# One pool of seven PSUM banks for scores, maxima and all other matmuls, in place of separate sets of two, two and three

## The chip, the cores and the metric

The kernel runs on one core of one Trainium2 chip. The metric is the device time of one execution in microseconds (us); lower is better. A core has a matrix engine (PE, whose weight loads are shown as PEld), a vector engine (DVE), a scalar engine (ACT), a general engine (POOL), DMA queues fed by SP, and an accumulation memory (PSUM) of eight banks, 512 fp32 values by 128 partitions each, that PE writes and DVE and ACT read.

## The reference, cut to what matters

Four blocks one after another work on `x` (4 batches, 256 rows, 160 columns) with a context of 512 rows of 96. Seven attentions are computed in all:

```python
x = L0(x, ctx)   # cross attention, 20 heads of 8, 512 keys
x = L1(x, ctx)   # LN, self attention (20 heads, 256 keys); LN, cross attention (512 keys); LN, gated feed forward 160 -> 2*640 -> 160
x = L2(x, ctx)   # 8 heads of 20: attention to 508 context rows, plus a small attention of 96 rows to x, fed to another with 4 keys
x = L3(x, ctx)   # as L1

# each attention
sim = einsum('bhid,bhjd->bhij', q, k) * scale
out = einsum('bhij,bhjd->bhid', softmax(sim), v)
```

## The kernel before, in words

**Staging.** The attentions make six phases (`PHASES`), each over four batches `b`. Within a phase and batch the heads are worked in groups of four, a *quad* (`quads`, 116 in all). For a quad with 512 keys the steps are:

- `max`, eight per quad: PE computes scores with queries as rows (one matmul of 512 columns, or two of 256 in self attention) into a bank `mx_ps` (line 911), and DVE reduces them to row maxima (line 1337). 720 in all.
- `negm`, then `mtr`: DVE negates the maxima (lines 1351 and 1352), PE transposes them (line 925), and DVE adds them to the queries as extra rows (line 1361), so that the next scores come out with the maximum subtracted.
- `st`, a *slot*, eight per quad: PE computes scores of two heads with keys as rows (two matmuls of 256 columns, line 889) into a bank `st_ps`, and ACT takes the exponential into one of eight `probs` buffers (line 1177). 736 in all.
- `pv`, four per quad: PE multiplies two slots' probabilities with the values into the bank `pv_ps` (eight matmuls of nine weight columns, line 949); `oev`: ACT copies the sum out (line 1186).

`max` and `st` use 64 of PE's 128 rows each: heads of one half of a quad lie on rows 0 to 63 and the others on rows 64 to 127, and two such matmuls of different halves run at the same time. `pv` splits the columns of PE into four. All other steps use the whole array: projections, transposes of keys and queries (`k_tr`, line 994; `q_tr`, line 1053), the way out of an attention (`o_nat`, `o_tr`, `o_proj`) and the feed forward (`ff_g`, `ff_a`, `ff_o`). There are 640 of these with a bank, the 116 `mtr` among them, and they take a bank in turn from three, `sp_ps`; ACT or DVE empties it.

**Banks.** `st_ps` has two banks (`N_ST`), `mx_ps` two (`N_MX`), `sp_ps` three (`N_SP`), each set used in strict rotation, and `pv_ps` one.

**What sets the order.** Nothing is ordered at run time: a planner (`simulate`) runs when the kernel is built and writes down one order of all 2,995 steps, which every engine then follows through its own queue, with semaphores between them. The planner keeps a clock per engine. At each point it takes, of the first steps of several streams (slots; maxima; `mtr`; `pv`; background work), the one that PE could start first, and between equal times the one with the earlier due time. It reckons 95 ns (`MODE`) for a change between the three shapes of PE (rows, columns, full), 210 ns (`HANDOFF`) from engine to engine, 60 + 1.05 ns a column for DVE and 60 + 0.834 ns a column for ACT. A step that needs a bank can't start before the planned end of the reader of the step before it in that bank. Maxima run some 8 to 16 slots ahead of the slots of their quad (`M_LEAD` is 8), and a slot also needs that the `pv` of eight slots before is done.

Of the kernel before, what the change touches and what calls it, by code (L numbers as in the profile page):

```python
# [62 lines left out]
N_ST = 2  # L63
N_SP = 3
N_MX = 2
# [132 lines left out]
def plan():  # L198
# [61 lines left out]
    order = simulate(quads, slots, due, stages)  # L260
    return order, quads, slots
# [103 lines left out]
def simulate(quads, slots, due, stages):  # L365
# [38 lines left out]
    def data_needs(step):  # L404
# [81 lines left out]
    done, order, uses, maxes = {}, [], [], []  # L486
# [3 lines left out]
    while any(heads) or any(stages) or any(map(any, active)) or any(active_low):  # L490
        for p in range(3):
            if not any(active[p]) and stages[p] and (stages[p][0][0] is None or stages[p][0][0] in done):
                active[p] = [list(x) for x in stages[p].pop(0)[1]]
        best = None
        for li in heads + active[0] + active[1] + active[2] + active_low:
            if not li:
                continue
            step = li[0]
            need = needs(step)
            if any(x not in done for x in need):  # L500
                continue
            lock = takes_buffer(step)
            if lock and held.get(lock[0]) not in (None, lock[1]):
                continue
            start = max([done[x] for x in need], default=0)
            if step[0] in SPARE and len(uses) >= N_SP:
                if uses[-N_SP] not in done:
                    continue
                start = max(start, done[uses[-N_SP]])
            if step[0] == "max" and len(maxes) >= N_MX:  # L510
                start = max(start, done[maxes[-N_MX]])
            key = (max(start, pe_free(step)), due.get(step)) if cost(step, quads)[0] else (max(start, clock["pe"]), (-10**6, 0, 0))
            if best is None or key < best[0]:
                best = (key, start, li, step)
        key, start, li, step = best
        li.pop(0)
        order.append(step)
        lock = takes_buffer(step)
        if lock:
            held[lock[0]] = None if lock[2] else lock[1]  # L520
        pe, after = cost(step, quads)
        t = start
        if pe:
            begin = max(start, pe_free(step))
            mode, t = shape(step), begin + pe
            if mode == "rows":
                lanes[lane(step)], clock["pe"] = t, begin + (pe / 2 if step[0] == "st" else 0)
            else:
                lanes, clock["pe"] = [t, t], t
        for eng, ns in after:  # L530
            t = clock[eng] = max(t + HANDOFF, clock[eng]) + ns
        done[step] = t + (DMA_LATENCY if step[0] == "kdma" else HANDOFF)
        if step[0] in LOW:

            uses.append(("low", step))
            active_low.append([("low", step)])
        elif step[0] in SPARE:
            uses.append(step)
        if step[0] == "max":
            maxes.append(step)  # L540
    return order
# [6 lines left out]

LOW = {"kv_proj", "qkv_proj", "q_proj", "ca_q"}
# [3 lines left out]
    "scores_full": {"st"}, "probs_ready": {"st"}, "max_full": {"max"}, "max_taken": {"max"}, "negm_ready": {"negm"},  # L553
# [19 lines left out]
def build(nc, io):  # L573
    order, quads, slots = plan()

    value, seen, turn, uses = {}, {}, {}, 0
    for step in order:
# [7 lines left out]
        if step[0] in SPARE:  # L585
            turn[step] = (uses % N_SP, uses // N_SP)
            uses += 1

    def slot_value(name, s):
        return value[name, ("st", s)]  # L590

    with ExitStack() as ctx:
# [6 lines left out]

        st_ps = [ctx.enter_context(nc.psum_tensor(f"st_ps{i}", [P, 512], F32)) for i in range(N_ST)]  # L600
        mx_ps = [ctx.enter_context(nc.psum_tensor(f"mx_ps{i}", [P, 512], F32)) for i in range(N_MX)]
        pv_ps = ctx.enter_context(nc.psum_tensor("pv_ps", [P, 512], F32))
        sp_ps = [ctx.enter_context(nc.psum_tensor(f"sp_ps{i}", [P, 512], F32)) for i in range(N_SP)]
# [69 lines left out]
        spare_full = [sem(f"spare_full{i}") for i in range(N_SP)]  # L673
        spare_taken = [sem(f"spare_taken{i}") for i in range(N_SP)]
# [65 lines left out]
        def taken(eng, step):  # L740

            b, k = turn[step]
            eng.wait_ge(spare_taken[b], k + 1)
# [19 lines left out]
        with nc.Block() as block:  # L763
# [31 lines left out]
            def _(pe):  # L795

                pe.wait_ge(s_warm, 1)
                for _ in range(WARM_UP):
                    pe.matmul(st_ps[0][:, :], probs[:, 0, 0:P], probs[:, 0, :], start=True, stop=True)
# [10 lines left out]
        with nc.Block() as block:  # L810
            @block.sync
            def _(sp):
# [14 lines left out]
                for step in order:  # L827
                    if step[0] == "kdma":
# [6 lines left out]
                        if before is not None:  # L835

                            sp.wait_ge(S["scores_full"], quads[before]["slots"][-1] + 1)
# [23 lines left out]
            def _(pe):  # L861
                def take(step):

                    b, k = turn[step]
                    if k:
                        pe.wait_ge(spare_taken[b], k)
                    return sp_ps[b], spare_full[b]
# [6 lines left out]
                for step in order:  # L874
                    kind = step[0]
                    if kind == "st":
# [7 lines left out]
                        if s >= N_ST:  # L884

                            pe.wait_ge(S["probs_ready"], slot_value("probs_ready", s - N_ST))
                        kr = chunk_rows(a["nk"], c)
                        for i, h in enumerate(sl["heads"]):
                            mm = pe.matmul(st_ps[s % N_ST][0:kr, i * a["nq"]:(i + 1) * a["nq"]],  # L889
                                           key_op(n, h)[:, c * P:c * P + kr], query_rows(u, b, h),  # L890
                                           start=True, stop=True)
                        mm.then_inc(S["scores_full"], 1)
                    elif kind == "max":
# [12 lines left out]
                        o = value["max_full", step] - 1  # L906
                        if o >= N_MX:
                            pe.wait_ge(S["max_taken"], o - N_MX + 1)
                        tt = 0 if t == TQ else t
                        for j, h in enumerate(heads):  # L910
                            mm = pe.matmul(mx_ps[o % N_MX][0:rows, j * a["nk"]:(j + 1) * a["nk"]],  # L911
                                           query_rows(u, b, h)[:, tt * P:tt * P + rows], key_op(n, h)[:, 0:a["nk"]],
                                           start=True, stop=True)
                        mm.then_inc(S["max_full"], 1)
# [13 lines left out]
                    elif kind == "pv":  # L928
# [8 lines left out]
                        pe.wait_ge(S["probs_ready"], slot_value("probs_ready", mine[-1]))  # L937
# [208 lines left out]
            def filled(eng, step):  # L1146

                b, k = turn[step]
                eng.wait_ge(spare_full[b], k + 1)
                return sp_ps[b], spare_taken[b]  # L1150
# [8 lines left out]
            def _(act):  # L1159
# [6 lines left out]
                for step in order:  # L1166
                    kind = step[0]
                    if kind == "st":
                        s = step[1]
                        a = ATT[slots[s]["u"]]  # L1170
                        act.wait_ge(S["scores_full"], s + 1)
                        if s >= N_P:
# [4 lines left out]
                        nc.scalar.activation(probs[0:kr, s % N_P, 0:w], st_ps[s % N_ST][0:kr, 0:w], ACT.Exp,  # L1177
                                             scale=float(a["dh"]) ** -0.5).then_inc(S["probs_ready"], 1)
# [30 lines left out]
                    elif kind == "x_keys":  # L1209
# [4 lines left out]
                        act.wait_ge(spare_full[turn[prev][0]], turn[prev][1] + 1)  # L1214
# [74 lines left out]
            def _(dve):  # L1289
# [38 lines left out]
                for step in order:  # L1328
                    kind = step[0]
                    if kind == "max":  # L1330
# [4 lines left out]
                        o = value["max_full", step]  # L1335
                        dve.wait_ge(S["max_full"], o)
                        nc.vector.tensor_reduce(mx[b][0:rows, t, heads[0]:heads[-1] + 1:heads[-1] - heads[0] or 1],  # L1337
                                                mx_ps[(o - 1) % N_MX][0:rows, 0:a["hpm"] * a["nk"]].rearrange("p (h k) -> p h k", k=a["nk"]),
                                                AX.X, ALU.max).then_inc(S["max_taken"], 1)
                    elif kind == "negm":  # L1340
# [6 lines left out]
                        dve.wait_ge(S["max_taken"], value["max_taken", ("max", n, len(quads[n]["items"]) - 1)])  # L1347
# [185 lines left out]
```

## Time and profile before

| | us |
|---|---|
| median of 3 runs (1029.38 to 1034.0) | 1033.69 |
| the profiled execution | 1032.42 |
| its span, first to last instruction | 1030.3 |
| PE busy | 975.2 |
| DVE busy | 680.7 |
| ACT busy | 672.4 |
| POOL busy | 55.1 |

Busy is the time in which an engine had at least one instruction under way. Matmuls are pipelined, and the end of each is modelled, so that short stops of PE lie inside its busy time; the start times of its instructions and the idle time of PEld tell more.

### The profile page before, as it was taken

What the parts mean: (1) busy time and instruction counts of PE and PEld (TensorE: products, weight loads), DVE (VectorE), ACT (ScalarE), POOL (GpSimd) and SP (SyncE); (2) the same over time, 40 slices, a digit from 0 to 9 for tenths busy, and PEclk for the clock granted to TensorE, in tenths of its full rate; (3) what the DMA queues carried; (4) which work ended last, traced back from release to release, by engine and by line L of the source; (5) the groups of instructions that cost most, each with busy time, mean ns of one, the idle gap of its engine ahead of it and who ended that gap; (6) DMA issues with size and microseconds to landing.
All of it is one profiled execution on the core that took longest, in us unless ns stands there. A gap on an engine that the chain in (4) does not pass through costs nothing.

```text
span 1030.3 us, 21206 instructions
## 1 busy us (share of the span) xinstructions
PE 975.2 (95%) x7808; PEld 642.1 (62%) x7808; DVE 680.7 (66%) x1607; ACT 672.4 (65%) x1416; POOL 55.1 (5%) x92
## 2 busy tenths in 40 slices
PE   4999999999999999999999999999999999989878
PEld 2865565566666657676667766665666666665636
DVE  2168878787776875757675677577587875848531
ACT  1567777676777677767776577576577775756541
POOL 2000000000000001000000000000000000000000
PEclk7589999999999999999999999799699998998975
DMA  7111111101112001011000300001011101011000
GB/s 182 45 24 42 24 30 42 25 23 24 27 26 48 22 22 32 22 32 32 12 2 2 78 1 1 22 17 26 18 26 42 35 19 38 22 33 26 18 1 6
DMA packets 25324, 30.04 MB, mean 29 GB/s; under 512 B 9204, under 2 KB 16824, under 8 KB 25064
## 3 DMA queue, kind: packets, MB, share of 16 engines
q1 hardware_dynamic: 25224, 28.69, 12.0%
q8 instruction: 64, 1.05, 0.4%
q14 instruction: 36, 0.29, 0.1%
HBM read 7.04 MB, written 0.66 MB: 7 GB/s over the span
## 4 chain that ended last, share of the span: by engine, by line
PE 87%; DVE 5%; issue 3%; ACT 2%; DMA 1%; SPq 0%; POOL 0%; ACTq 0%; DVEq 0%; POOLq 0%
PE pv_ps L949 18%; PE mx_ps L911 16%; PE st_ps L889 13%; PE sp_ps L871 8%; PE sp_ps L872 7%; PE sp_ps L994 6%; PE sp_ps L976 4%; PE sp_ps L925 4%; PE sp_ps L1053 3%; DVE mx L1337 3%; PE sp_ps L1065 3%; PE sp_ps L1104 2%; ACT probs L1177 1%; DMA ctx_n<-in_ctx 1%; PE sp_ps L1011 1%
## 5 line engine op out<-in xcount | busy, mean ns | idle before, releaser
L1337 DVE TENSOR_REDUCE mx<-mx_ps 128x1 f32<-128x512 f32 (+3 forms) x720 | 465.9, 684 | 151.2 <-PE mx_ps L911 148.5
L1177 ACT ACTIVATE probs<-st_ps 128x512 f32<-128x512 f32 x736 | 395.3, 587 | 149.1 <-PE st_ps L889 142.6
L911 PE MATMUL mx_ps<-ring,qT 64*128 64x512 f32 (+1 forms) x800 | 221.0, 435 | 11.9 <-issue 6.6
L949 PE MATMUL pv_ps<-probs,v 128*9 128x256 f32 (+2 forms) x2944 | 225.4, 391 | 1.1 <-ACT oT L1186 0.7
L889 PE MATMUL st_ps<-qT,ring 64*128 64x256 f32 x1280 | 208.9, 309 | 6.2 <-ACT probs L1177 2.9
L889 PEld LDWEIGHTS st_ps<-qT,ring 64*128 64x128 f32 x1280 | 152.8, 191 | 48.9 <-ACT probs L1177 30.7
L911 PEld LDWEIGHTS mx_ps<-ring,qT 64*128 64x128 f32 x800 | 103.3, 193 | 108.5 <-DVE mx L1337 52.0
L949 PEld LDWEIGHTS pv_ps<-probs,v 128*9 128x9 f32 (+2 forms) x2944 | 50.5, 91 | 62.2 <-issue 17.7
L1228 ACT ACTIVATE kdense<-sp_ps 128x512 fp32r<-128x512 f32 (+2 forms) x116 | 59.2, 542 | 24.1 <-PE sp_ps L994 23.3
L994 PE MATMUL sp_ps<-identr,ks 128*128 128x128 f32 (+1 forms) x416 | 68.3, 299 | 0.1
L994 PEld LDWEIGHTS sp_ps<-identr,ks 128*128 128x128 f32 (+1 forms) x416 | 58.1, 207 | 12.0 <-issue 8.9
L1186 ACT ACTIVATE oT<-pv_ps 128x256 f32<-128x256 f32 x108 | 41.6, 385 | 30.5 <-PE pv_ps L949 30.3
L1361 DVE TENSOR_TENSOR qT<-sp_ps,qT 128x256 fp32r<-128x256 f32 (+1 forms) x108 | 47.0, 435 | 20.1 <-PE sp_ps L925 20.0
L1164 ACT ACTIVATE ks<-sp_ps 128x320 fp32r<-128x320 f32 x80 | 35.5, 443 | 35.4 <-PE sp_ps L872 17.7
L1303 DVE TENSOR_TENSOR ks<-sp_ps,ks 128x160 fp32r<-128x160 f32 x80 | 24.1, 316 | 50.0 <-ACT v L1200 39.6
L925 PEld LDWEIGHTS sp_ps<-identr,mn 128*128 128x128 f32 (+1 forms) x248 | 38.7, 199 | 28.0 <-issue 23.5
L925 PE MATMUL sp_ps<-identr,mn 128*128 128x128 f32 (+1 forms) x248 | 53.9, 306 | 1.1 <-DVE mn L1352 1.0
L871 PE MATMUL sp_ps<-hT_out,wb 80*128 80x256 f32 x160 | 53.7, 420 | 1.2 <-ACT hT_out L1238 1.2
L872 PE MATMUL sp_ps<-hT_out,wb 80*128 80x256 f32 x160 | 52.2, 411 | 0.0
L1469 POOL TENSOR_SCALAR rstd<-mv 128x2 f32<-128x2 f32 x24 | 5.2, 217 | 802.9 <-DVE mv L1375 802.9
L1411 DVE TENSOR_TENSOR x<-sp_ps,xb 128x320 f32<-128x320 f32 x32 | 15.7, 491 | 43.3 <-PE sp_ps L872 22.5
L1053 PE MATMUL sp_ps<-identr,qs 128*128 128x128 f32 (+1 forms) x248 | 42.0, 304 | 0.0
(151 smaller groups left out, 1094.4 us busy)
## 6 DMA issues: line engine op xcount, KB each, us to landing
ring<-kdense SPq DMA_DIRECT2D x240, 64.0 KB, 2.0
ring<-kdense SPq DMA_DIRECT2D x160, 32.0 KB, 1.8
wb<-in_w_blk SPq DMA_DIRECT2D x2, 1400.0 KB, 9.1
wd<-in_w_down SPq DMA_DIRECT2D x2, 400.0 KB, 9.6
ctx_n<-in_ctx SPq DMA_DIRECT2D x4, 192.0 KB, 2.6
x<-in_x SPq DMA_DIRECT2D x4, 160.0 KB, 2.9
bias<-in_bias SPq DMA_DIRECT2D x1, 640.0 KB
out_rows<-x SPq DMA_DIRECT2D x4, 160.0 KB, 1.9
```

Source lines behind the costliest of these rows:

```text
L871: pe.matmul(out, lhs[:, 0, :], rhs[:, 0, :], start=True, stop=False)
L872: return pe.matmul(out, lhs[:, 1, :], rhs[:, 1, :], start=False, stop=True)
L889: mm = pe.matmul(st_ps[s % N_ST][0:kr, i * a["nq"]:(i + 1) * a["nq"]], key_op(n, h)[:, c * P:c * P + kr], query_rows(u, b, h), start=True, ...
L911: mm = pe.matmul(mx_ps[o % N_MX][0:rows, j * a["nk"]:(j + 1) * a["nk"]], query_rows(u, b, h)[:, tt * P:tt * P + rows], key_op(n, h)[:, 0:a ...
L925: mm = pe.matmul(bank[:, k * a["nq"] + i * P:k * a["nq"] + i * P + rows], m, identr[0:rows, 0:rows], start=True, stop=True)
L949: mm = pe.matmul(pv_ps[32 * j:32 * j + a["dh"] + 1, 0:a["nq"]], v, probs[0:kr, s % N_P, i * a["nq"]:(i + 1) * a["nq"]], start=(c == 0), st ...
L994: mm = pe.matmul(bank[:, k * SQ + t * P:k * SQ + t * P + kr], ks[0:kr, t, g * of(u):(g + 1) * of(u), :].rearrange("p h s -> p (h s)"), ide ...
L1053: mm = pe.matmul(bank[:, k * nq + i * P:k * nq + i * P + rows], query_stack(u, b)[0:rows, t, g * of(u):(g + 1) * of(u), :].rearrange("p h ...
L1177: nc.scalar.activation(probs[0:kr, s % N_P, 0:w], st_ps[s % N_ST][0:kr, 0:w], ACT.Exp, scale=float(a["dh"]) ** -0.5).then_inc(S["probs_rea ...
L1228: nc.scalar.activation(dst, bank[:, 0:n * SQ].rearrange("p (g k) -> p g k", g=n)[:, :, 0:w], ACT.Copy).then_inc(free, 1)
L1337: nc.vector.tensor_reduce(mx[b][0:rows, t, heads[0]:heads[-1] + 1:heads[-1] - heads[0] or 1], mx_ps[(o - 1) % N_MX][0:rows, 0:a["hpm"] * a ...
L1361: nc.vector.tensor_tensor(q, bank[:, 0:(g1 - g0) * nq], q.bitcast(F32), ALU.add).then_inc(done, 1)
```

## The change

The three sets of banks become one pool of seven. Every step that writes a bank other than `pv` (`BANKED`) may take any of the seven. Which one is no longer a rotation: the planner keeps the last user of each bank, and for a step it looks at the banks whose last user has been planned. Of those that by its clock are free when the step could start anyway, it takes the one freed last; if none is free by then, the one that comes free first, and the step starts then. The bank of each step (`place`) is handed on with the order, each bank has its own pair of semaphores for full and taken, and the waits of `st`, `max` and `pv` use these. The requirement that slot `s` waits for the exponential of slot `s - 2`, and a maximum for the reduction two before, is gone. Since the planner's choice depends on the banks, the order of all steps changes as well. Costs, due times, streams and the instructions of each step stay as they are.

```diff
-N_ST = 2
-N_SP = 3
-N_MX = 2
+N_BANK = 7
...
-            return [("mtr", slots[s]["n"])] + ([("st", s - N_ST)] if s >= N_ST else []) + ([pv_of[s - N_P]] if s >= N_P else [])
+            return [("mtr", slots[s]["n"])] + ([pv_of[s - N_P]] if s >= N_P else [])
...
-    done, order, uses, maxes = {}, [], [], []
+    done, order, place = {None: 0}, [], {}
+    banks = N_BANK * [None]
...
-            if step[0] in SPARE and len(uses) >= N_SP:
-                if uses[-N_SP] not in done:
+            bank = None
+            if step[0] in BANKED:
+                free_at = [(done[x], i) for i, x in enumerate(banks) if x in done]
+                if not free_at:
                     continue
-                start = max(start, done[uses[-N_SP]])
-            if step[0] == "max" and len(maxes) >= N_MX:
-                start = max(start, done[maxes[-N_MX]])
+                ready = [(t, i) for t, i in free_at if t <= max(start, pe_free(step))]
+                t, bank = max(ready) if ready else min(free_at)
+                start = max(start, t)
...
+        if bank is not None:
+            banks[bank] = ("low", step) if step[0] in LOW else step
+            place[step] = bank
+    return order, place
...
+BANKED = SPARE | {"st", "max"}
...
-        if step[0] in SPARE:
-            turn[step] = (uses % N_SP, uses // N_SP)
-            uses += 1
...
+        if step[0] in BANKED:
+            turn[step] = (place[step], uses[place[step]])
+            uses[place[step]] += 1
...
-                        if s >= N_ST:
-
-                            pe.wait_ge(S["probs_ready"], slot_value("probs_ready", s - N_ST))
+                        bank, full = take(step)
...
-                        mm.then_inc(S["scores_full"], 1)
+                        mm.then_inc(full, 1)
...
-                        o = value["max_full", step] - 1
-                        if o >= N_MX:
-                            pe.wait_ge(S["max_taken"], o - N_MX + 1)
+                        bank, full = take(step)
...
-                        pe.wait_ge(S["probs_ready"], slot_value("probs_ready", mine[-1]))
+                        taken(pe, ("st", mine[-1]))
```

## Rows read from the trace of the kernel before

**Rows 1.** Page: span, busy time of each engine, granted PE clock in 40 slices
```profile
span 1030.3 us, 21206 instructions
PE 975.2 (95%) x7808; PEld 642.1 (62%) x7808; DVE 680.7 (66%) x1607; ACT 672.4 (65%) x1416; POOL 55.1 (5%) x92
...
PEclk7589999999999999999999999799699998998975
```

**Rows 2.** Page: the chain that ended last, shares of the span by engine
```profile
PE 87%; DVE 5%; issue 3%; ACT 2%; DMA 1%; SPq 0%; POOL 0%; ACTq 0%; DVEq 0%; POOLq 0%
```

**Rows 3.** Waits: who waited for whom, us in total, times, longest
```profile
DVE mx L1337 <- PE mx_ps L911: 148.5, 204, 4.5
ACT probs L1177 <- PE st_ps L889: 142.6, 207, 3.9
...
PEld mx_ps L911 <- DVE mx L1337: 54.1, 131, 0.8
...
PEld st_ps L889 <- ACT probs L1177: 34.0, 85, 0.9
...
PEld st_ps L889 <- DVE qT L1361: 3.0, 7, 0.5
```

**Rows 4.** Timeline of PE from 498 us: start, length, line, count of matmuls
```profile
500.13 0.62 PE L949 MATMUL pv_ps<-probs,v 128*9 128x256 f32 x8
500.68 0.49 PE L911 MATMUL mx_ps<-ring,qT 64*128 64x512 f32 x1
501.08 0.50 PE L889 MATMUL st_ps<-qT,ring 64*128 64x256 f32 x2
501.43 0.40 PE L911 MATMUL mx_ps<-ring,qT 64*128 64x512 f32 x1
501.57 0.50 PE L889 MATMUL st_ps<-qT,ring 64*128 64x256 f32 x2
502.00 0.62 PE L949 MATMUL pv_ps<-probs,v 128*9 128x256 f32 x8
502.55 0.38 PE L889 MATMUL st_ps<-qT,ring 64*128 64x256 f32 x1
...
503.21 0.62 PE L949 MATMUL pv_ps<-probs,v 128*9 128x256 f32 x8
```

**Rows 5.** Timeline of PE: two maxima alone, and sixteen `pv` matmuls in one
```profile
155.73 0.50 PE L911 MATMUL mx_ps<-ring,qT 64*128 64x512 f32 x2
156.16 0.62 PE L949 MATMUL pv_ps<-probs,v 128*9 128x256 f32 x8
...
302.99 1.05 PE L949 MATMUL pv_ps<-probs,v 128*9 128x256 f32 x16
303.97 0.51 PE L911 MATMUL mx_ps<-ring,qT 64*128 64x256 f32 x4
```

**Rows 6.** Timeline: first and last of the blocks of maxima and slots
```profile
49.45 0.79 PE L911 MATMUL mx_ps<-ring,qT 64*128 64x512 f32 x2
...
992.52 0.98 PE L889 MATMUL st_ps<-qT,ring 64*128 64x256 f32 x4
```

**Rows 7.** Groups by line: busy us, mean ns of one, idle before
```profile
L1337 DVE TENSOR_REDUCE mx<-mx_ps 128x1 f32<-128x512 f32 (+3 forms) x720 | 465.9, 684 | 151.2 <-PE mx_ps L911 148.5
L1177 ACT ACTIVATE probs<-st_ps 128x512 f32<-128x512 f32 x736 | 395.3, 587 | 149.1 <-PE st_ps L889 142.6
...
L1228 ACT ACTIVATE kdense<-sp_ps 128x512 fp32r<-128x512 f32 (+2 forms) x116 | 59.2, 542 | 24.1 <-PE sp_ps L994 23.3
...
L1361 DVE TENSOR_TENSOR qT<-sp_ps,qT 128x256 fp32r<-128x256 f32 (+1 forms) x108 | 47.0, 435 | 20.1 <-PE sp_ps L925 20.0
```

**Rows 8.** PE idle before lines 911 and 889 itself, by releaser
```profile
PE mx_ps L911 <- DVE mx L1337: 5.0, 12, 0.5
...
PE st_ps L889 <- ACT probs L1177: 3.1, 8, 0.7
```

**Rows 9.** Windows: us, busy PE, PEld, DVE, ACT, POOL (instructions), granted clock, DMA share, GB/s
```profile
60.00:210.00 150.00, 146.06 (x1233) 86.07 (x1233) 119.06 (x260) 106.76 (x221) 5.27 (x9) 1.00 0.13 30
210.00:510.00 300.00, 293.66 (x2517) 194.46 (x2517) 217.94 (x522) 217.49 (x456) 15.79 (x26) 0.99 0.12 27
510.00:760.00 250.00, 242.63 (x2034) 166.41 (x2033) 167.08 (x427) 166.57 (x375) 14.02 (x23) 0.92 0.08 19
760.00:985.00 225.00, 213.05 (x1718) 138.58 (x1717) 154.22 (x348) 147.71 (x294) 11.37 (x18) 0.95 0.12 28
```

**Rows 10.** Timeline of PE: part of a feed forward at full clock, eight matmuls
```profile
504.52 0.59 PE L872 MATMUL sp_ps<-hT_out,wb 80*128 80x256 f32 x2
...
506.25 0.59 PE L872 MATMUL sp_ps<-hT_out,wb 80*128 80x256 f32 x2
```

**Rows 11.** Timeline: the start of steady work and the way out of the last attention
```profile
24.14 1.09 PE L963 MATMUL sp_ps<-ident,ctx_n 128*96 128x128 f32 x4 [12.42 <-DMA ctx_n<-in_ctx]
...
994.91 0.38 ACT L1186 ACTIVATE oT<-pv_ps 128x256 f32<-128x256 f32 x1 [0.77 <-PE pv_ps L949]
...
1027.46 0.49 DVE L1411 TENSOR_TENSOR x<-sp_ps,xb 128x320 f32<-128x320 f32 x1 [2.99 <-PE sp_ps L1104]
```

More of the change, by code:

```diff
@@ L259, in plan @@
         put(s, -1, ("st", s))
-    order = simulate(quads, slots, due, stages)
-    return order, quads, slots
+    order, place = simulate(quads, slots, due, stages)
+    return order, place, quads, slots
 def takes_buffer(step):
@@ L573, in build @@
 def build(nc, io):
-    order, quads, slots = plan()
-    value, seen, turn, uses = {}, {}, {}, 0
+    order, place, quads, slots = plan()
+    value, seen, turn, uses = {}, {}, {}, N_BANK * [0]
     for step in order:
@@ L597, in sem @@
             return ctx.enter_context(nc.semaphore(name))
[L600 to L601 removed]
         pv_ps = ctx.enter_context(nc.psum_tensor("pv_ps", [P, 512], F32))
[L603 removed]
+        bank_ps = [ctx.enter_context(nc.psum_tensor(f"bank_ps{i}", [P, 512], F32)) for i in range(N_BANK)]
         wm = sb("wm", [DH, 2, 640])
@@ L672, in build @@
         S = {name: sem(name) for name in SIGNALS}
-        spare_full = [sem(f"spare_full{i}") for i in range(N_SP)]
-        spare_taken = [sem(f"spare_taken{i}") for i in range(N_SP)]
+        bank_full = [sem(f"bank_full{i}") for i in range(N_BANK)]
+        bank_taken = [sem(f"bank_taken{i}") for i in range(N_BANK)]
         ring_in = [sem(f"ring_in{i}") for i in range(RING)]
@@ L798, in _ @@
                 for _ in range(WARM_UP):
-                    pe.matmul(st_ps[0][:, :], probs[:, 0, 0:P], probs[:, 0, :], start=True, stop=True)
+                    pe.matmul(bank_ps[0][:, :], probs[:, 0, 0:P], probs[:, 0, :], start=True, stop=True)
             @block.gpsimd
@@ L835, in _ @@
                         if before is not None:
-                            sp.wait_ge(S["scores_full"], quads[before]["slots"][-1] + 1)
+                            at_b, k = turn["st", quads[before]["slots"][-1]]
+                            sp.wait_ge(bank_full[at_b], k + 1)
                         for j in range(4):
@@ L1170, in _ @@
                         a = ATT[slots[s]["u"]]
-                        act.wait_ge(S["scores_full"], s + 1)
+                        bank, free = filled(act, step)
                         if s >= N_P:
@@ L1176, in _ @@
                         w = a["hps"] * a["nq"]
-                        nc.scalar.activation(probs[0:kr, s % N_P, 0:w], st_ps[s % N_ST][0:kr, 0:w], ACT.Exp,
-                                             scale=float(a["dh"]) ** -0.5).then_inc(S["probs_ready"], 1)
+                        nc.scalar.activation(probs[0:kr, s % N_P, 0:w], bank[0:kr, 0:w], ACT.Exp,
+                                             scale=float(a["dh"]) ** -0.5).then_inc(free, 1)
                     elif kind == "oev":
@@ L1334, in _ @@
                         t, rows, heads = quads[n]["items"][i]
-                        o = value["max_full", step]
-                        dve.wait_ge(S["max_full"], o)
+                        bank, free = filled(dve, step)
                         nc.vector.tensor_reduce(mx[b][0:rows, t, heads[0]:heads[-1] + 1:heads[-1] - heads[0] or 1],
-                                                mx_ps[(o - 1) % N_MX][0:rows, 0:a["hpm"] * a["nk"]].rearrange("p (h k) -> p h k", k=a["nk"]),
-                                                AX.X, ALU.max).then_inc(S["max_taken"], 1)
+                                                bank[0:rows, 0:a["hpm"] * a["nk"]].rearrange("p (h k) -> p h k", k=a["nk"]),
+                                                AX.X, ALU.max).then_inc(free, 1)
                     elif kind == "negm":
@@ L1346, in _ @@
                         t0, t1, rows = tiles[0][0], tiles[-1][0] + 1, tiles[0][1]
-                        dve.wait_ge(S["max_taken"], value["max_taken", ("max", n, len(quads[n]["items"]) - 1)])
+                        taken(dve, ("max", n, len(quads[n]["items"]) - 1))
                         m = mx[b][0:rows, t0:t1, 4 * qd:4 * qd + 4]
```

32 lines of the change are left out of this document (12 added, 20 removed).

## The prediction

> **What bounds the kernel now.** I read the page's shares first. PE has something under way in 95% of the span, DVE in 66% and ACT in 65% [rows 1], and the chain that ended last lies on PE for 87% of the time and on DVE for 5% [rows 2]. So PE sets the pace, but a busy PE is not a PE that streams columns. Two things hide in its 975.2 us.
>
> The first is the change of shape. In the timeline, sixteen `pv` matmuls in one block take 303.97 - 302.99 = 0.98 us and eight take 0.55 us (502.55 - 502.00) [rows 4, 5]. Eight more cost 0.43, so a `pv` block has a fixed cost of 0.12. Two maxima alone take 156.16 - 155.73 = 0.43 [rows 5], although 512 columns at 2.4 GHz stream in 0.21 and the two halves of the array work side by side; a block with two maxima and two slots takes 503.21 - 502.55 = 0.66 [rows 4]. Two more slots cost 0.23, so a block of maxima and slots has a fixed cost of 0.22. Over the whole trace I count 398 blocks of maxima and slots, the first at 49.45 us and the last at 992.52 [rows 6], 315 `pv` blocks and 250 blocks of full-array work. The fixed cost of the first two kinds is 398 x 0.22 + 315 x 0.12 = 88 + 38 = 126 us.
>
> The second is short stops for a bank. PEld stood 131 times, 54.1 us, until DVE had read a bank of maxima, and 85 times, 34.0 us, until ACT had read a bank of scores: 88.1 us over 216 gaps, 0.41 each [rows 3]. The block from 500.68 to 502.00 shows it: maximum, slot, maximum, slot, each waiting for the bank of the one before, 1.32 us for what takes 0.66 two blocks later [rows 4]. PE's own idle time shows only 5.0 + 3.1 = 8.1 us of this [rows 8], because a modelled matmul end covers the rest. Each gap also covers a block's fixed cost, which is already counted: 88.1 - 216 x 0.22 = 41 us is my reading of the true stops, between 8.1 and 88.1.
>
> Of the 398 blocks, 205 hold exactly two slots and two maxima of one matmul each, and 72 the same in self attention, where a maximum has two matmuls. In 277 of 398, then, the block ends where both pairs of banks are spent. That is the evidence that banks end blocks.
>
> **The change, part by part.**
>
> *Longer blocks.* Maxima and slots had four banks. Now they have seven less what the other work holds. That work has 640 steps in the 925 us from 60 to 985. PE writes such a bank in about 0.4, the reader takes 0.542 (a copy of keys) or 0.435 us (adding maxima to queries) [rows 7], and two hand-offs lie between. I put it at 1.4 us a step, so 640 x 1.4 / 925 = 1.0 bank is held on average. Six are left, and a block could be 1.5 times as long: 133 fewer of the 398 and, as `pv` runs wait for the same slots, about 100 fewer of the 315. That is worth 133 x 0.22 + 100 x 0.12 = 41 us. It is the upper bound, since the planner takes whatever can start first, and a bank that comes free every 0.6 us brings PE back early for a small block. The lower bound is nothing. I take two thirds, nearer the upper because 277 blocks end at the limit: **-27 us**.
>
> *Stops for a bank.* With more banks the planner can place another step where it now places one that must wait. It can't remove those that come from its own clock being off: a reduction takes 684 ns in the trace [rows 7] and 60 + 1.05 x 512 = 598 in its books, an exponential 587 against 487. I take half of the 41: **-20 us**, between 0 and -88.
>
> *Longer stretches of full-array work.* Staying in the same shape costs the planner no 95 ns, so full-array work wins every tie while it has banks. A feed forward step is eight matmuls, 506.25 - 504.52 = 1.73 us [rows 10]. With three banks a run of them ends after three; with seven, `ff_g` and `ff_a` of one batch can run together: three more steps, the last of half the size, 1.73 + 1.73 + 0.86 = 4.3 us, while no slot or maximum starts. In eight feeds that is 34 us in which DVE and ACT run dry. PE does needed work meanwhile, so only what DVE or ACT can't catch up counts. DVE is busy in 119.06 of 150 us (79%) from 60 to 210, and 67 to 73% later, where the feeds are [rows 9]. It catches up at about 30%. I charge a quarter, **+8 us**, between 0 and +34.
>
> *Waits.* `st`, `max` and `pv` have as many waits as before, on other semaphores. The copies into `ring` wait for the same slot as before. No instruction is added, and the extra maxima in flight lie behind the cover that the due times give (8 slots of 925 / 736 = 1.26 us are 10 us; three more reductions ahead of line 1361 are 2.1 us). If that cover were gone, slots would wait for `qT`, 3.0 us in 7 gaps now [rows 3], and 2.1 us in each of 116 quads would be 240 us; nothing in the trace is near that.
>
> *Start and end.* Until 60 us and after 994.91 the order is a chain in which banks play little part: from the last copy-out of `pv` to the last addition is 1027.46 - 994.91 = 33 us [rows 11]. I cost both at nothing. The granted clock is 0.92 of full from 510 to 760 [rows 9], in pieces after stops of PE; fewer stops may give some us back and longer ones may take some, which I leave at zero, plus or minus 8.
>
> Sum: -27 - 20 + 8 = -39 us. The profiled execution took 1032.42 us, of which 1030.3 is span; that gives 993.4. The median of the runs is 1.3 us above the profiled one, which changes nothing here. I forecast **993 us**.
>
> **The rivals.**
>
> *A. Reading the banks sets the pace, and blocks stay as short as they are.* A block then ends because ACT and DVE have not read, and more banks only lengthen the queue. For it: PE comes back with 736 slots in 925 us, one per 1.26 us, and an exponential takes 0.587, a reduction 0.684 [rows 7]; the planner, always taking the earliest start, would fill each bank as it comes free. Against it: DVE waits 148.5 us for maxima and ACT 142.6 us for scores [rows 3], so they are not the ones that are late. It gives 1032, and with a part of the stops gone down to 1015. The Trainium skill (TensorEngine Tiling, Performance Considerations, "PSUM Bottleneck") says that tiling speeds up PE but not the reading of PSUM, which may become the limit. By that rule the time would stay near 1032; the trace agrees only in part, with DVE at 79% in its fullest stretch.
>
> *B. Banks that the planner believes free are not.* This one is slower. The pool hands out the bank freed last by the planner's clock, not the one free longest, so a step stands on the most recent planned end even where an older bank lies idle. A reduction is 86 ns longer than planned and an exponential 100. With two banks a reader can be 0.2 us behind its plan; after a queue of seven it is 0.6 us. Of 736 + 720 + 640 = 2096 uses, a new stop of 0.2 us at one in five is 419 x 0.2 = 84 us, and the time 993 + 84 = 1077; at one in eight, 1045. It decides from 235 new stops of 0.2 us (47 us) on. Against it: PE is itself slower than planned (0.22 fixed in place of 0.095 in each of 398 blocks, 50 us in all), which gives the readers time.
>
> *C. Full-array work crowds out the slots.* The term of +8 becomes +34 and blocks gain nothing: 1032 + 34 - 20 = 1046. For it stands the tie rule; against it the share of DVE after 210 us.
>
> *D. Most of both costs goes.* -41 for the blocks and all 41 of the stops: 950.
>
> **How the numbers follow.** About 0.5% is what a measurement of this kernel can tell from no change (its runs lie 1029.38 to 1034.0); within 0.5% of 1033.7 means 1028.5 to 1038.9. Chances: my forecast, 975 to 1015, 0.48; D, under 975, 0.13; A 0.20, of which 0.08 lies from 1015 to 1028.5 and 0.12 within 0.5%; B 0.12; C 0.07, both slower. So faster 0.48 + 0.13 + 0.08 = 0.69, same 0.12, slower 0.19. The range runs from 960, which leaves out less than 0.1 of D, to 1045, which leaves out most of B and part of C: 960 to 1045. The likeliest case alone has 975 to 1015.
>
> **What the profile after would show.** Right: some 265 to 310 blocks of maxima and slots in place of 398, many with three or more slots; gaps of PEld before `max` and `st` for DVE and ACT down from 88 to under 60 us; DVE near 690 of a span of 991, 69%; runs of feed forward matmuls longer than 5.2 us. A shows as many blocks as now. B shows more and shorter gaps of PEld with the same busy times. C shows feed forward runs near 9 us with DVE idle beside them, and gaps before the `max` that follow. What would make the forecast wrong is above all the order itself: it comes out of a greedy rule that no row of before shows for seven banks.

## The result, and the profile after

The change makes the kernel 4.5% slower: 1079.67 us median of 4 runs (1070.7 to 1083.11) against 1031.54 us (1029.15 to 1034.0); the ratio is 1.0453 with a 95% interval of 1.0381 to 1.0525. I had forecast 993 us, 4% faster, and a range up to 1045. In some of the kernels below a part of the executions was over 1.5% slower than the fastest of the same kernel, at a lower granted clock; medians are of all executions, and ratios leave those out. I use the ratios where two kernels are compared, and 1031.5 us times the ratio where a sum is made.

The page of the kernel after: span, busy time, granted PE clock in 40 slices, and the chain by engine.

```profile
span 1081.3 us, 21205 instructions
PE 996.3 (92%) x7808; PEld 674.2 (62%) x7808; DVE 668.5 (62%) x1607; ACT 653.5 (60%) x1416; POOL 55.4 (5%) x92
...
PEclk8659998999989998888969999576999899789995
...
PE 76%; DVE 8%; ACT 8%; issue 5%; DMA 1%; SPq 0%; POOL 0%; ACTq 0%; DVEq 0%; POOLq 0%
```

The work is the same; DVE and ACT are busy a little less than before, in a span that is 51 us longer [rows 1]. PE is busy only 21 us more. The chain has changed most: DVE and ACT had 7% of it between them [rows 2] and have 16% now. And the clock line has many more figures below 9. Time at the lower of the two clock levels (1.2 GHz) follows from the mean granted clock: 2 x (1 - 0.934) x 1030.3 = 136 us before, 2 x (1 - 0.886) x 1081.3 = 247 us after.

Waits of the kernel after (`max` is line 905 now, `st` line 885, `pv` line 943), which answer to [rows 3]:

```profile
ACT probs L1171 <- PE bank_ps L885: 147.3, 125, 5.0
DVE mx L1330 <- PE bank_ps L905: 109.7, 112, 4.5
ACT kdense L1222 <- PE bank_ps L988: 65.2, 40, 7.7
...
PEld bank_ps L885 <- ACT probs L1171: 18.0, 47, 1.0
PEld bank_ps L885 <- DVE qT L1354: 17.4, 16, 2.5
...
PEld bank_ps L885 <- DVE mx L1330: 11.3, 36, 0.5
...
PEld bank_ps L905 <- ACT probs L1171: 10.5, 30, 0.8
...
PEld bank_ps L905 <- DVE mx L1330: 8.5, 19, 0.8
```

Gaps of PEld for a bank of scores or maxima fell from 88.1 us in 216 to 18.0 + 11.3 + 10.5 + 8.5 = 48.3 us in 132, as forecast. The reader looks at the other side: ACT waits 1.18 us at a time for scores (147.3 / 125) where it waited 0.69 (142.6 / 207), and for copies of keys (line 1222) up to 7.7 us. Slots now stand 17.4 us for the maxima in `qT` (3.0 before).

Windows of the kernel after, in the columns of [rows 9]; the last one is a stretch that is looked at next:

```profile
60.00:210.00 150.00, 140.58 (x1187) 84.28 (x1186) 110.00 (x245) 97.84 (x211) 5.29 (x9) 0.92 0.13 30
210.00:510.00 300.00, 277.56 (x2298) 188.45 (x2294) 198.91 (x480) 193.07 (x416) 14.07 (x23) 0.92 0.11 26
510.00:760.00 250.00, 237.18 (x1804) 165.13 (x1804) 142.35 (x366) 147.39 (x337) 12.36 (x20) 0.84 0.06 15
760.00:985.00 225.00, 214.40 (x1795) 145.07 (x1796) 160.17 (x386) 152.83 (x326) 11.44 (x19) 0.93 0.13 29
426.00:443.00 17.00, 17.00 (x68) 14.53 (x68) 3.40 (x8) 5.00 (x12) 0.86 (x1) 0.60 0.01 1
```

From 510 to 760 us DVE falls from 67% to 57% of the time and the clock from 0.92 to 0.84 (the kernel after is some us behind there, so that the two windows do not hold quite the same steps). Timeline of PE of the kernel after, around 426 us:

```profile
422.26 2.63 PE L885 MATMUL bank_ps<-qT,ring 64*128 64x256 f32 x9
425.55 0.62 PE L943 MATMUL pv_ps<-probs,v 128*9 128x256 f32 x8 [0.66 <-ACT probs L1171]
426.10 0.64 PE L919 MATMUL bank_ps<-identr,mn 128*128 128x128 f32 x2
426.54 1.16 PE L869 MATMUL bank_ps<-hT_out,wb 80*128 80x256 f32 x2
...
434.32 1.06 PE L870 MATMUL bank_ps<-hT_out,wb 80*128 80x256 f32 x2
434.82 2.16 PE L988 MATMUL bank_ps<-identr,ks 128*128 128x128 f32 x8
436.78 4.44 PE L1098 MATMUL bank_ps<-wd,gate 128*128 128x160 f32 x20
440.95 0.44 PE L988 MATMUL bank_ps<-identr,ks 128*128 128x128 f32 x2
441.23 1.29 PE L970 MATMUL bank_ps<-wbc,ctxT 96*128 96x320 f32 x4
...
442.89 0.62 PE L943 MATMUL pv_ps<-probs,v 128*9 128x256 f32 x8
```

and ACT in the same stretch:

```profile
425.87 2.56 ACT L1171 ACTIVATE probs<-bank_ps 128x512 f32<-128x512 f32 x5
436.16 0.60 ACT L1222 ACTIVATE kdense<-bank_ps 128x512 fp32r<-128x512 f32 x1 [7.73 <-PE bank_ps L988]
```

This is one stretch of full-array work of 442.89 - 426.10 = 16.8 us: an `mtr`, `ff_a` and `ff_o` of one feed forward, transposes of keys, context projections and transposes of rows, steps of several chains, with no slot and no maximum between. PE is busy for all 17 us, DVE for 3.4 and ACT for 5.0. Before it stand nine score matmuls that took 2.63 us, since their weight loads waited for DVE to read maxima, and then a wait for ACT:

```profile
423.79 0.29 PEld L885 LDWEIGHTS bank_ps<-qT,ring 64*128 64x128 f32 x2 [0.30 <-DVE mx L1330]
424.39 0.29 PEld L885 LDWEIGHTS bank_ps<-qT,ring 64*128 64x128 f32 x2 [0.30 <-DVE mx L1330]
425.55 0.12 PEld L943 LDWEIGHTS pv_ps<-probs,v 128*9 128x9 f32 x8 [0.87 <-ACT probs L1171]
```

The granted clock was 1.00 in those 4 us with waits and 0.51 in the 14 us of unbroken work behind them:

```profile
422.00:426.00 4.00, 2.96 (x23) 1.59 (x19) 2.69 (x6) 3.96 (x6) 0.00 (x0) 1.00 0.28 65
426.00:440.00 14.00, 14.00 (x47) 12.11 (x44) 2.66 (x6) 3.63 (x7) 0.00 (x0) 0.51 0.01 1
```

Counted over each trace between 60 us and the last 50: 21 full-array stretches of over 4 us before, 102 us in all, the longest 6.3; after, 36 of 255 us, the longest 16.8.

Blocks by the same count: 398 of slots and maxima before and 258 after; `pv` 315 and 229; full-array 250 and 148.

### The profile page after: what moved, and what is told of

Read it like the earlier page. It is cut to its first block, busy times and chain, and to the rows that moved or that the text cites. A ratio compares the mean times of both kernels' runs of the same rounds, so it can differ in the third digit from the quotient of the medians.

```text
span 1081.3 us, 21205 instructions
## 1 busy us (share of the span) xinstructions
PE 996.3 (92%) x7808; PEld 674.2 (62%) x7808; DVE 668.5 (62%) x1607; ACT 653.5 (60%) x1416; POOL 55.4 (5%) x92
## 4 chain that ended last, share of the span: by engine, by line
PE 76%; DVE 8%; ACT 8%; issue 5%; DMA 1%; SPq 0%; POOL 0%; ACTq 0%; DVEq 0%; POOLq 0%
PE pv_ps L943 15%; PE bank_ps L885 10%; PE bank_ps L905 10%; PE bank_ps L869 9%; PE bank_ps L870 8%; DVE mx L1330 6%; PE bank_ps L988 5%; ACT probs L1171 5%; PE bank_ps L970 4%; PE bank_ps L919 3%; PE bank_ps L1059 3%; PE bank_ps L1047 3%; PE bank_ps L1098 3%; ACT oT L1180 1%; DMA ctx_n<-in_ctx 1%
## 5 line engine op out<-in xcount | busy, mean ns | idle before, releaser
L1330 DVE TENSOR_REDUCE mx<-bank_ps 128x1 f32<-128x512 f32 (+3 forms) x720 | 448.5, 682 | 110.4 <-PE bank_ps L905 109.7
L1171 ACT ACTIVATE probs<-bank_ps 128x512 f32<-128x512 f32 x736 | 377.4, 604 | 149.1 <-PE bank_ps L885 147.3
L885 PE MATMUL bank_ps<-qT,ring 64*128 64x256 f32 x1280 | 177.4, 321 | 17.1 <-DVE qT L1354 9.9
L885 PEld LDWEIGHTS bank_ps<-qT,ring 64*128 64x128 f32 x1280 | 132.9, 197 | 81.2 <-issue 29.7
L905 PE MATMUL bank_ps<-ring,qT 64*128 64x512 f32 (+1 forms) x800 | 164.7, 412 | 7.4 <-issue 3.1
L905 PEld LDWEIGHTS bank_ps<-ring,qT 64*128 64x128 f32 x800 | 86.9, 196 | 59.2 <-issue 29.1
L988 PE MATMUL bank_ps<-identr,ks 128*128 128x128 f32 (+1 forms) x416 | 66.8, 309 | 1.9 <-DVE mx L1330 1.0
L988 PEld LDWEIGHTS bank_ps<-identr,ks 128*128 128x128 f32 (+1 forms) x416 | 60.1, 219 | 8.4 <-DVE mx L1330 2.7
L869 PE MATMUL bank_ps<-hT_out,wb 80*128 80x256 f32 x160 | 60.6, 467 | 1.4 <-ACT hT_out L1232 1.2
L870 PE MATMUL bank_ps<-hT_out,wb 80*128 80x256 f32 x160 | 59.1, 458 | 0.0
L919 PE MATMUL bank_ps<-identr,mn 128*128 128x128 f32 (+1 forms) x248 | 57.7, 322 | 1.4 <-DVE mx L1330 0.8
```

The costliest lines, as they stand in the source:

```text
L869: pe.matmul(out, lhs[:, 0, :], rhs[:, 0, :], start=True, stop=False)
L870: return pe.matmul(out, lhs[:, 1, :], rhs[:, 1, :], start=False, stop=True)
L885: mm = pe.matmul(bank[0:kr, i * a["nq"]:(i + 1) * a["nq"]], key_op(n, h)[:, c * P:c * P + kr], query_rows(u, b, h), start=True, stop=True)
L905: mm = pe.matmul(bank[0:rows, j * a["nk"]:(j + 1) * a["nk"]], query_rows(u, b, h)[:, tt * P:tt * P + rows], key_op(n, h)[:, 0:a["nk"]], st ...
L919: mm = pe.matmul(bank[:, k * a["nq"] + i * P:k * a["nq"] + i * P + rows], m, identr[0:rows, 0:rows], start=True, stop=True)
L988: mm = pe.matmul(bank[:, k * SQ + t * P:k * SQ + t * P + kr], ks[0:kr, t, g * of(u):(g + 1) * of(u), :].rearrange("p h s -> p (h s)"), ide ...
```

## The experiments

All are variants of the changed kernel; the planner makes the order, so a change of its rules is a change of order alone. Each was timed beside the kernel before on the same chip.

**E1. Order of before, seven banks, longest-free bank.** Limits per kind are back in the planner, the bank is another.

```diff
+CAPS = {'st': 2, 'max': 2, 'full': 3}
...
+                mine = held_by[step[0] if step[0] in ("st", "max") else "full"]
+                cap = CAPS[step[0] if step[0] in ("st", "max") else "full"]
+                if len(mine) >= cap:
+                    if mine[-cap] not in done:
+                        continue
+                    start = max(start, done[mine[-cap]])
...
-                t, bank = max(ready) if ready else min(free_at)
+                t, bank = min(ready) if ready else min(free_at)
```

> The order of before, step for step (full-array steps at most three banks, slots two, maxima two, as before in the planner), but each step takes, of seven banks, the one longest free. Only the banks differ from before, so waits for a bank should all but vanish: the 88.1 us of PEld gaps before maxima and slots fall below 20. If the slowdown of the change lies in the order, this runs as before or a little faster: 1005 to 1032 us. If it lies in the seven-bank pool itself (semaphores, another way of sharing banks between ACT, DVE and PE), this is slower than before, towards 1080.

Measured: 988.9 us, ratio 0.9576 (0.9534 to 0.9617): 4.2% faster than before, and below the range of the expectation. Sharing the banks is good; the slowdown comes from the order or from the choice of bank. Page and waits of this run (`max` is line 914, `st` line 894):

```profile
span 988.8 us, 21206 instructions
PE 925.4 (94%) x7808; PEld 606.2 (61%) x7808; DVE 674.6 (68%) x1607; ACT 667.3 (67%) x1416; POOL 55.2 (6%) x92
```

```profile
PEld bank_ps L914 <- issue: 94.9, 232, 3.6
...
PEld bank_ps L914 <- DVE mx L1339: 2.2, 7, 0.4
PEld bank_ps L894 <- DVE mx L1339: 1.9, 8, 0.4
...
PEld bank_ps L894 <- ACT probs L1180: 0.5, 2, 0.3
```

Waits for a bank went from 88.1 us to under 5. The gaps before `max` did not vanish: they are put down to "issue" now, 94.9 us where that was 52.1 before. I read them as the fixed cost of a block, which the waits had covered; no run shows that apart. What fell is the time from the first matmul of a block to the next block: 347 us for the 398 blocks of slots and maxima before, 315 here, with the same contents. One wait grew: weight loads of slots stood for the maxima in `qT` 10.7 us in 25 gaps, where it was 3.0 in 7 [rows 3].

**E2. Order of the change, longest-free bank.**

```diff
-                t, bank = max(ready) if ready else min(free_at)
+                t, bank = min(ready) if ready else min(free_at)
```

> The order of the changed kernel, step for step, but of the banks that the planner holds free, the one longest free is taken and not the one freed last. Rival B (banks that the planner believes free are not) expects most of the loss to go: about 1040 us or less, with gaps of PEld clearly shorter. The theory that the order is at fault expects 1065 to 1082 us, as the changed kernel, with the granted clock still near 0.89.

Measured: 1059.91 us, ratio 1.0262 (1.0219 to 1.0306). The choice of bank is worth 1080 - 1059 = some 20 us in this order, so rival B is real (1060 lies between the two expectations); the order alone, at the same choice of bank, costs 1.0262 against 0.9576, 71 us.

The traces of E1 and E2 show where. From the first matmul of a block to the next block, blocks of slots and maxima take 315 us in E1 and 360 in E2, full-array blocks 433 and 456, `pv` blocks 204 and 200. The lower clock level holds for 106 us in E1 and 184 in E2. If such time counts half, an estimate of what the work would take at the higher level, full-array blocks take 408 us in E1 and 406 in E2, no more, and blocks of slots and maxima 305 and 341. So by this estimate the full-array stretches lose nothing inside but the clock; the rest is paid in the blocks of slots and maxima. It is not paid only right behind the stretches of over 4 us: for 1000 columns of slots and maxima, again with the lower level counted half, E2 takes 0.46 us in the 10 us behind such a stretch and 0.46 elsewhere, E1 0.45 and 0.40.

**E3 and E4. Which kind may not spread.** As the change, with `CAPS` of (99, 99, 3) in E3 and (2, 2, 99) in E4 for slots, maxima and full-array steps, and the bank freed last.

> The pool of seven, but the full-array steps may hold three banks at most, as before; slots and maxima have no limit of their own. If full-array work that crowds out slots and maxima costs the 48 us (rival C), most of them come back: 1015 to 1045 us, with stretches of full-array work above 8 us gone or rare, and the granted clock back at 0.92 or more. If it is the blocks of one kind (slots alone or maxima alone, up to six or eight), little comes back: 1060 to 1080.

> The other half: slots and maxima hold two banks each at most, as before, and only the full-array steps may take all the rest. If full-array work is what costs, this is as slow as the changed kernel or slower: 1070 to 1110 us, with the clock below 0.90. If blocks of one kind are what costs, this is near before: 1025 to 1045.

Measured: E3 1031.8 us, ratio 1.0003 (0.9974 to 1.0033); E4 1105.18 us, ratio 1.0608 (1.0513 to 1.0703). Holding full-array work to three banks gives 46 us back; freeing full-array work alone is at least as slow as the whole change (the intervals just touch, and the ratio of E4 rests on two executions). Free slots and maxima are not the main fault. Two things came out otherwise than expected. In E3 the clock did not come back (0.904 to 0.915), and the stretches of over 4 us still make 149 us, the longest 13.0, where 255 us and 16.8 were counted after the change. In E4 the clock is higher than after the change (0.902 to 0.923 against 0.886 to 0.896) and the kernel no faster, so the clock can't be all of the loss; and its order is 3% longer than that of before even by the planner's own clock.

**E5. Order of before, bank freed last.** E1 with the change's own choice, `max(ready)`.

> The order of before, step for step, on the pool of seven, but with the change's own choice of bank: the one freed last by the planner's clock. The run with the longest-free bank took 989. If the choice of bank costs by itself (rival B), this lies near 1005 to 1030, and PEld gaps for DVE and ACT before maxima and slots come back to 40 to 90 us; if it costs only in the new order, this is near 989.

Measured: 1037.93 us, ratio 1.0084 (1.0032 to 1.0136), against 0.9576 for E1: 52 us from the choice of bank alone, in an order that is the same step for step, and more than the expectation had (1005 to 1030). All that the pool gives is lost, and a little more. The waits for a bank are back:

```profile
PEld bank_ps L914 <- DVE mx L1339: 32.6, 78, 0.8
PEld bank_ps L894 <- ACT probs L1180: 32.1, 79, 0.9
PEld bank_ps L914 <- ACT probs L1180: 22.7, 54, 1.5
```

By the planner's own clock, 49% of the uses of a bank start within 0.2 us of the time at which it comes free in E5, and 2% in E1. In the order of the change it is 51% with the bank freed last and 33% in E2.

**E6. E3 with the longest-free bank.**

> Both at once: the order of the run in which full-array work holds three banks at most (1032), but each step in the longest-free bank. If the choice of bank costs some 20 us in any order, 1005 to 1020; if the two causes overlap, 1025 to 1032. If it is still well above 989, what is left is the limit of two that slots and maxima had.

Measured: 1008.38 us, ratio 0.982 (0.9751 to 0.9888). Against E3, 19 us for the choice of bank; against E2, 46 us for the limit of three; against E1, 25 us are left to the free slots and maxima.

**E7 and E8. Three banks each; and the planner's costs nearer the trace.** `CAPS` of (3, 3, 3), longest-free bank; E8 has also

```diff
-    act = lambda *ns: [("act", sum(60 + 0.834 * n for n in ns))]
-    dve = lambda *ns: [("dve", sum(60 + 1.05 * n for n in ns))]
+    act = lambda *ns: [("act", sum(150 + 0.834 * n for n in ns))]
+    dve = lambda *ns: [("dve", sum(150 + 1.05 * n for n in ns))]
...
-MODE = 95
+MODE = 160
```

> Slots, maxima and full-array work hold three of the seven banks each at most, longest-free bank. The planner's own clock puts its order 3% shorter than the one of before. If bursts of one kind were what hurt and moderate limits keep the three shapes mixed, 960 to 985 us, below the 989 of the old order. If the old order is better than anything that the planner finds by longer blocks, 990 to 1020.

> As the run before, with the planner's costs nearer the trace: 150 ns in place of 60 fixed for each DVE and ACT instruction, 160 in place of 95 for a change of shape. If part of the stops comes from the planner's clock being off, 5 to 20 us less than the run before; otherwise the same within 10.

Measured: E7 1006.19 us, ratio 0.9819 (0.9725 to 0.9912); E8 0.9854 (0.9804 to 0.9904), with a median of 1026.48 over 11 executions. Neither beats E1, though both make longer blocks (346 blocks of slots and maxima in E7) and the planner's own clock has the order of E7 3% shorter than that of before; the better costs gave nothing that can be told apart, where 5 to 20 us were expected if the planner's clock was at fault. E8 shows something else: its executions run from 1005.94 us at a mean clock of 0.932 to 1042.43 at 0.893, one program with one order.

**E9. No limits, but short stretches.**

```diff
+            if cost(step, quads)[0] and mode == "full" and shape(step) == "full" and stretch >= STRETCH:
+                key = (key[0] + 2000, key[1])
             if best is None or key < best[0]:
...
+            stretch = (stretch if mode == "full" else 0) + pe if shape(step) == "full" else 0
```

`STRETCH` is 3500 ns; the rest is E2.

> The planner of the changed kernel, no limit on the banks of any kind, longest-free bank, and one rule added: once full-array work has run for 3.5 us on end by the planner's clock, its next step is held 2 us back in the choice, so that slots, maxima or pv come first if they can. Against the run with the same bank choice and no such rule (1060 us). If the long stretches themselves cost (slots and maxima left out, ACT and DVE dry), it takes 1005 to 1030, like the limit of three banks did (1008). If what costs is that full-array steps hold banks that slots need, it stays at 1045 to 1060.

Measured: 1008.17 us, ratio 0.9789 (0.9711 to 0.9868), against 1.0262 for E2: 49 us back with no limit on anyone's banks. The page of this run:

```profile
span 1005.3 us, 21206 instructions
PE 944.2 (94%) x7808; PEld 642.6 (64%) x7808; DVE 663.5 (66%) x1607; ACT 651.9 (65%) x1416; POOL 55.3 (6%) x92
```

Its longest full-array stretch is 8.4 us (16.8 in E2), and the stretches of over 4 us make 178 us (232 in E2). In the planned order full-array steps hold four or more banks for 99 us and up to seven at once, in E2 for 87 us and up to six. So it is not the banks that full-array steps hold; what a limit on the length of their stretches changes in the order is what counts. Blocks of slots and maxima take 326 us here, 360 in E2; with the time at the lower level counted half, 305, as in E1. One reservation: the rule moves other steps too, all through the order, and by the planner's own clock this order is 31 us shorter than that of E2. That each long stretch by itself costs its share is not shown.

**E10. Order of before, slots and maxima in four common banks, full-array work in three.**

> The order of before, step for step. Slots and maxima take the longest-free of four banks in common, full-array steps the longest-free of three, as before. The run in which all seven are in common took 989, separate sets 1031. If what helps is that slots and maxima no longer stand behind their own two readers, most of the 43 us is here: 990 to 1005. If it needs the full-array steps' idle banks as slack, 1015 to 1030.

Measured: 1021.2 us, ratio 0.991 (0.9857 to 0.9962). A fifth of what E1 gained. The rest needs all seven in common, that is, the banks that full-array work leaves idle. The expectation had left both cases open; the time is in the range of the second.

**E11. The limits of before and the rule of E9.** `CAPS` of (2, 2, 3), longest-free bank, `STRETCH` of 3500.

> The limits of before (two, two, three) and the pool of seven with the longest-free bank, as in the fastest run so far (989), and the rule of 3.5 us for full-array stretches added, which changes the order somewhat. If long stretches cost in that order too, 975 to 987; if its stretches are short enough (21 of 4 us and more), 985 to 1000, no different from another order of the same kind.

Measured: 1001.06 to 1048.77 us in four executions, the profiled one at a mean clock of 0.91. All four are above the 975 to 1000 of the expectation. No ratio could be formed, and nothing follows but that it is not plainly better than E1.

**E12. Order of before, bank freed last, with a margin of 1 us.** E5 with

```diff
+                ready = [x for x in ready if x[0] <= max(start, pe_free(step)) - 1000]
                 t, bank = max(ready) if ready else min(free_at)
```

> The order of before, step for step, pool of seven, and again the bank freed last, but only among banks that the planner's clock has free for at least 1 us; if there is none, the longest-free one. Same order as the runs of 989 (longest free) and 1038 (freed last). If the freed-last choice costs because the planner's books are off by some tenths of a us, so that the reader is not done yet, 1 us of margin gives it all back: 985 to 1000. If it costs for another reason (uneven use of the banks, say), it stays at 1015 to 1038.

Measured: 988.0 us, ratio 0.9605 (0.9528 to 0.9681), the same as E1. The bank freed last costs because the reader is often not done at the time in the planner's books; 1 us of margin cures it whole, with a bank free for 1.08 us in the median before its next use by the plan, and 0.21 in E5.

## Why the prediction was wrong

By ratio, from 1031.5 us: the pool in the old order with the longest-free bank -44 (E1); the new order on top of it +71 (E2); the bank freed last on top of that +20. The sum is +47.

**Longer blocks, -27: right in the count, not seen in the time.** I forecast 265 to 310 blocks and got 258; `pv` fell by 86 where I said about 100. At my fixed costs that is 140 x 0.22 + 86 x 0.12 = 41 us, my upper bound. No run shows them saved: the 258 blocks take 363 us from start to start where the 398 took 347, and no kernel with fewer blocks ran below 1003 us, where E1, with 398, takes 989. By the planner's own clock, too, the new order is no shorter than the old one (892.8 us against 890.5), which could have been read before anything ran. A long run of slots waits inside the block, as the x9 above does, for 2.63 us.

**Stops for a bank, -20: mis-sized, and put to the wrong cause.** My reading of the true stops, 41 us, was near: E1 removes them with an unchanged order and gains 44. That is partly luck, since E1 also has 30 us less at the lower level (106 against 136), worth up to 15; the blocks of slots and maxima, where the stops were, fell by 32. I halved it because half seemed to come from the planner's wrong clock. The pool with spare banks cures those too, and the choice of bank undoes it.

**Longer stretches of full-array work, +8, between 0 and +34: this is the step that failed.** The rule was seen (no 95 ns to stay, so full-array work wins the ties), but I looked only at the feed forward, at 4.3 us more in eight places, and charged a quarter since DVE had 30% to spare. The trace shows that unlike steps link up, 36 stretches and 255 us in place of 21 and 102, up to 16.8 us. Two ways of cutting them give back 46 us (E6 against E2) and 49 us (E9 against E2). DVE's slack on average did not help: the blocks of slots and maxima behind the stretches take 341 us in E2 and 305 in E1 and E9, at the higher clock level by the estimate above. I had read that as PE waiting, behind each stretch, for a DVE and an ACT that have run dry. That fits the one stretch shown, but the extra time lies as much elsewhere (0.46 us for 1000 columns in both places in E2), so that this reading is not shown as the cause of all of it. This was rival C, which I gave 0.07: its mechanism was right, and its upper price of 34 us too low.

**Rival B, slower, 0.12: under-rated.** I priced it at 0.2 us a stop with a decision point of 47 us. Its place and its sign were right, it takes 52 us in the old order (E5 against E1) and 20 in the new (the change against E2), and E12 shows the cause. That its 1077 lies beside the measured 1080 is luck: it had the blocks gained in full and 84 us of new stops. I treated it as a rival that excludes my forecast, but it is a term beside the others, and of the size of the -47 that I had for blocks and stops together.

**Clock, 0 plus or minus 8: a second term that was mis-sized.** 110 us more ran at the lower level. Full-rate work of that length would lose up to 55 us. What the clock costs can be estimated from executions of one order. The kernel before, timed beside E9, ran from 1018.2 us at a mean clock of 0.951 to 1033.38 at 0.932, 8 us for each 0.01, and those of E3 lie 10.5 us apart for 0.011. By 8 us for 0.01, the change (0.891 in the mean of four) loses some 35 of its 48 us against the kernel before (0.935) with the clock, and E2 (0.906) some 35 of its 71 against E1 (0.949). These are not beside the terms above but a part of them, since the limits on the stretches bring a part of the clock back too (0.928 in E6, 0.917 in E9). The other half of the 71 is waiting, in the blocks of slots and maxima. What makes the clock fall is open in part. Stops for a bank alone move it little: in one order, with the bank freed last and the one longest free, it is 0.891 and 0.906 (the change, E2), 0.940 and 0.949 (E5, E1). The order moves it by 0.043 (E1, E2). It fell to 0.51 in the stretch shown, right behind stops of PE, and to 0.53 in the same stretch of E2 (416 to 430 us); whether such stretches or the stops around them do it, no run separates. The Trainium skill (TensorE: Matmul & The Clock Gate, "A second HAM failure mode: psum-queue depth-cycling") tells of a kernel in which short idle times between groups of matmuls make the clock swing between its two levels; the trace after agrees in that the clock changes between its levels more often, with 9 of the 40 slices of the clock line below 9 before and 17 after, but the runs in one order say that stops for a bank are a small part of the reason.

**Start and end, at nothing: 8 us.** The first block of slots or maxima starts 2.7 us later than before, and the last one 5.8 us further from the end.

**Rival A is out.** The rule of the Trainium skill that I set beside it (TensorEngine Tiling, "PSUM Bottleneck") is not what limits here: E1 gains 4.2% with the same readers.

What stays open besides what makes the clock fall: the last 25 us between E6 and E1, which I put to blocks of one kind without having shown it. E7, with three banks each, did not get them back.

## What to carry to other kernels

When a resource feeds a planner, test the resource and the order apart: the same order on the new banks gained 4.2%, and the order that the new banks let the planner choose lost more. A greedy rule that takes what can start first needs a limit on how long one kind may run, as 46 to 49 us for two such limits show: PE was busy for all of a stretch of 17 us in which DVE had work for 3.4. A planner's own total for the new order is there before anything runs: here it showed no gain. A good total is not enough, though, since those of E7 and E9 were 3% shorter than that of E1, and both ran longer. And a buffer chosen by planned times should be the one longest free, or have a margin above the error of the plan.

## What the runs showed of the hardware

I had not expected one program to spread so far: eleven executions of E8 lie between 1005.94 us at a mean clock of 0.932 and 1042.43 us at 0.893, 3.6%. A PE that is busy throughout can run at the lower level: the 14 us from 426 us after the change are PE 14.00 busy at a granted clock of 0.51. And a gap of PEld that ends by a semaphore says little of what the wait cost: in E1 the waits went from 88.1 to 5 us, the gaps before `max` moved to "issue" (52.1 us before, 94.9 here), and where time was saved (32 us in the blocks of slots and maxima) could be read only from the starts of the blocks.
